# A kernel of cross-attention and experts: when two of its last eight batches are loaded, and which engine issues five of the final stores

## The chip, the cores and the metric

The kernel runs on one core of a Trainium2 chip, in one launch. The metric is the device time of that launch in microseconds (us). The engines of the core work side by side, each through its own list of instructions: TensorE (PE), VectorE (DVE), ScalarE (ACT), GpSimd (POOL) and SyncE (SP), which here only issues DMA transfers. ScalarE and GpSimd issue transfers too. An engine waits on semaphores, and what stands behind a waiting instruction in its list waits with it.

## The reference

The input x has 16 batches of 256 rows with 256 columns. First it gets cross-attention on a normalised x, then a layer of eight experts, of which each row uses two:

```python
x = x + xattn(layernorm(x), ctx, ctx, Wq, bq, Wk, bk, Wv, bv)
h = layernorm(x)                        # 4096 rows of 256
logits = h @ Wr.T + br                  # 8 experts
vals, idx = top_k(logits, 2); w = softmax(vals)
out = 0
for e in range(8):
    y = gelu(h @ W1[e].T + b1[e]) @ W2[e].T + b2[e]     # 256 -> 1024 -> 256
    out = out + (w where idx == e, summed)[:, None] * y
z = out + h
z = (z - mean(z)) * rsqrt(var(z) + 1e-12) * ln_w + ln_b  # per row
x = x + z
```

## The kernel before

**Stages.** Up to about 200 us the kernel does the attention batch by batch, normalises, routes each row to its two experts, and writes h to two tables in DRAM: `tokens_dram`, from which rows are gathered, and `sums_dram`, on which the experts' outputs are added. Then come 39 blocks (`BLOCKS`), each of 256 rows of one expert, seven of them with only 128. For each block GpSimd gathers its rows with an indirect DMA (`fetch`), TensorE multiplies by W1 (`up`) and W2 (`down`) with weights split in high and low halves, ScalarE applies the gelu, VectorE splits and scales, and GpSimd adds the rows of the result to `sums_dram` with two indirect DMAs, 128 rows each (`give`, L646 to L660), here called scatters. A block's scatters wait until those of the block before have landed (`scattered[0]` counts even blocks, `scattered[1]` odd ones; `landed(m, p)` is the count when all blocks of parity p ahead of pair m are there).

**The last normalisation.** A batch of 256 rows is complete when all blocks with rows of it have been added. The full blocks are taken in an order that goes by their first rows, so low batches are complete early: batches 0 to 7 (`ON_TIME` = 8) are loaded back, normalised and stored beside the last blocks (`load_early` and `store_early`, L503 to L511); an assertion at L256 bounds, with `OPEN`, how many seats can still be open. Batches 8 to 15 come after the last block. Their place `z_all` lies over the memory of w1hi.

**The tail, engine by engine.** SyncE waits for all down-products and all scatters (L530 to L532), issues eight loads, at most four in flight (L533 to L535), then the store of batch 7 (L536). VectorE measures mean and variance of two batches at a time (`measure_z`, L1462: four statistics at L1466, four aggregations at L1470). GpSimd makes a scale and a shift of them (`norm_pair`, L710: L712, L713, L715, L718). ScalarE applies them and writes to PSUM (`normal`, L1149, two instructions a batch). VectorE multiplies by ln_w (`weigh`, L1475) and x is added: for batches 8 to 12 (`HANDED` = 5) by GpSimd (`finish`, L722), for 13 to 15 by VectorE (`finish`, L1480). ScalarE issues all eight stores (L1158), each as soon as four more batches have been normalised, and the last four at the end; before each it waits for its batch's finish.

The order on each engine is written out by hand. GpSimd: `norm_pair` 0, 1, 2, finish 8, `norm_pair` 3, finish 9 to 12. VectorE: measure pairs 0, 1, 2, weigh 8 and 9, measure pair 3, weigh 10 to 13, then finish and weigh in turn.

Of the kernel before, what the change touches and what calls it, by code (L numbers as in the profile page):

```python
# [27 lines left out]
P = 128  # L28
# [5 lines left out]
def at_least(eng, sem, n):  # L34

    if not (isinstance(n, int) and n <= 0):
        eng.wait_ge(sem, n)
# [10 lines left out]
def build(nc, x, ctx_in, Wq, bq, Wk, bk, Wv, bv, Wr, br, W1, b1, W2, b2, ln_w, ln_b, out):  # L48
    NB, SQ, D = x.shape
    SK = ctx_in.shape[1]  # L50
    E, FF, _ = W1.shape
# [7 lines left out]
    BT = TB * P  # L59
    FULL = TOPK * TOK // BT  # L60
    SHORT = E - 1
    BLOCKS = FULL + SHORT
# [2 lines left out]
    PAIR_OF = E * PER_EXPERT // TB  # L65
    FAR = 1 << 20
    NOWHERE = 99
    OPEN = E * (BT - 1) + SHORT * P
    ON_TIME = 8
    ON_TIME_AT = 11  # L70
    HANDED = 5
# [9 lines left out]
    out_v = out.rearrange("b (j p) d -> p b j d", p=P)  # L81
# [6 lines left out]
    with ExitStack() as stack:  # L88
# [3 lines left out]
        def sem(name):  # L92
            return stack.enter_context(nc.semaphore(name))

        def sem2(name):
            return [sem(f"{name}{i}") for i in range(2)]
# [128 lines left out]
        z_all = w1hi[:, :].bitcast(F32).rearrange("p (b j d) -> p b j d", b=NB, j=TJ)  # L225
# [27 lines left out]
        HB = len(f_h)  # L253
        SETTLED = (FIRST + SHORT + 1) // 2
        assert ON_TIME_AT + ON_TIME == BLOCKS // 2
        for i in range(ON_TIME):  # L256
            assert 2 * SQ * (NB - i - 1) >= BT * (BLOCKS - 2 * (ON_TIME_AT + i) + 1) + OPEN

        def tiles(m, p):

            return 1 if isinstance(m, int) and FIRST <= 2 * m + p < FIRST + SHORT else TB

        def landed(m, p):

            if isinstance(m, int):
                return 16 * sum(tiles(i, p) for i in range(m))
            return 16 * TB * m - 16 * len([j for j in range(FIRST, FIRST + SHORT) if j % 2 == p])
# [76 lines left out]
        h_mm = sem("h_mm")  # L344
# [3 lines left out]
        y_mm = sem("y_mm")  # L348
        y_ready = sem("y_ready")
        y_self = sem("y_self")  # L350
        scattered = sem2("scattered")
# [7 lines left out]
        o_ready = sem("o_ready")  # L359
        last_done = sem("last_done")  # L360
        stored = sem("stored")
# [60 lines left out]
        def _(sp):  # L422
# [86 lines left out]
            def store_early(i):  # L509
                sp.wait_ge(early_done, i + 1)  # L510
                sp.dma_start(out_v[:, i, :, :], x1[:, i, :, :]).then_inc(stored, 16)  # L511
# [15 lines left out]
                if p == 1 and 0 <= m - ON_TIME_AT < ON_TIME - 1:  # L527
                    store_early(m - ON_TIME_AT)

            sp.wait_ge(y_mm, HB * BLOCKS)  # L530
            sp.wait_ge(scattered[0], landed(BLOCKS // 2 + 1, 0))
            sp.wait_ge(scattered[1], landed(BLOCKS // 2, 1))  # L532
            for b in range(ON_TIME, NB):  # L533
                at_least(sp, sums_loaded[b % 4], 16 * ((b - ON_TIME) // 4))
                sp.dma_start(z_all[:, b, :, :], sums_v[:, b, :, :]).then_inc(sums_loaded[b % 4], 16)  # L535
            store_early(ON_TIME - 1)  # L536
            sp.wait_ge(stored, 16 * NB)


        @block.gpsimd  # L540
        def _(pool):
# [168 lines left out]
            def norm_pair(q):  # L710
                pool.wait_ge(stats3, q + 1)
                nc.gpsimd.tensor_scalar(nmu3[:, q, :], mv3[:, q, :, 0], -1.0, None, ALU.mult)  # L712
                nc.gpsimd.tensor_scalar(ve3[:, q, :], mv3[:, q, :, 1], EPS_FFN, None, ALU.add).then_inc(norm3_self, 1)  # L713
                pool.wait_ge(norm3_self, 2 * q + 1)
                nc.gpsimd.tensor_tensor(scale3[:, q, :], ve3[:, q, :],  # L715
                                        minus_half[:, :, :].rearrange("p w j -> p (w j)"), ALU.pow).then_inc(norm3_self, 1)
                pool.wait_ge(norm3_self, 2 * q + 2)
                nc.gpsimd.tensor_tensor(shift3[:, q, :], nmu3[:, q, :], scale3[:, q, :], ALU.mult).then_inc(rn3_ready, 1)  # L718

            def finish(b):  # L720
                pool.wait_ge(zw_ready, b - ON_TIME + 1)
                nc.gpsimd.tensor_tensor(z_all[:, b, :, :], z_all[:, b, :, :], x1[:, b, :, :], ALU.add).then_inc(o_ready, 1)  # L722

            norm_pair(0)
            norm_pair(1)
            norm_pair(2)
            finish(ON_TIME)
            norm_pair(3)
            for b in range(ON_TIME + 1, ON_TIME + HANDED):
                finish(b)  # L730


# [265 lines left out]
        def _(act):  # L998
# [145 lines left out]
            def normal(b):  # L1144
                q = (b - ON_TIME) // 2
                act.wait_ge(rn3_ready, q + 1)
                for j in range(TJ):
                    i = TJ * (b % 2) + j
                    ins = nc.scalar.activation(bank[b - ON_TIME][:, j * D:(j + 1) * D], z_all[:, b, j, :], ACT.Identity,  # L1149
                                               bias=shift3[:, q, i:i + 1], scale=scale3[:, q, i:i + 1])  # L1150
                ins.then_inc(zn_ready, 1)

            def store(b):
                if b < ON_TIME + HANDED:
                    act.wait_ge(o_ready, b - ON_TIME + 1)
                else:
                    act.wait_ge(last_done, b - ON_TIME - HANDED + 1)
                act.dma_start(out_v[:, b, :, :], z_all[:, b, :, :]).then_inc(stored, 16)  # L1158

            for b in range(ON_TIME, NB):  # L1160
                normal(b)
                if b >= ON_TIME + 4:
                    store(b - 4)
            for b in range(NB - 4, NB):
                store(b)


# [1 line left out]
        def _(dve):  # L1169
# [292 lines left out]
            def measure_z(q):  # L1462
                for b in (ON_TIME + 2 * q, ON_TIME + 2 * q + 1):
                    dve.wait_ge(sums_loaded[b % 4], 16 * ((b - ON_TIME) // 4 + 1))
                    for j in range(TJ):
                        ins = nc.vector.bn_stats(st3[:, q, TJ * (b % 2) + j, :], z_all[:, b, j, :])  # L1466
                ins.then_inc(z_self, 1)
                dve.wait_ge(z_self, q + 1)
                for i in range(PT):
                    ins = nc.vector.bn_aggr(mv3[:, q, i, :], st3[:, q, i, :])  # L1470
                ins.then_inc(stats3, 1)

            def weigh(b):
                dve.wait_ge(zn_ready, b - ON_TIME + 1)
                nc.vector.tensor_tensor(z_all[:, b, :, :], bank[b - ON_TIME][:, :].rearrange("p (j d) -> p j d", j=TJ),  # L1475
                                        lnw_bc[:, :].unsqueeze(1).to_broadcast([P, TJ, D]), ALU.mult).then_inc(zw_ready, 1)

            def finish(b):
                dve.wait_ge(zw_ready, b - ON_TIME + 1)
                nc.vector.tensor_tensor(z_all[:, b, :, :], z_all[:, b, :, :], x1[:, b, :, :], ALU.add).then_inc(last_done, 1)  # L1480

            measure_z(0)
            measure_z(1)
            measure_z(2)
            weigh(ON_TIME)
            weigh(ON_TIME + 1)
            measure_z(3)
            for b in range(ON_TIME + 2, ON_TIME + HANDED + 1):
                weigh(b)
            for b in range(ON_TIME + HANDED, NB):  # L1490
                finish(b)
# [29 lines left out]
```

## Time and profile before

| what | value |
| --- | --- |
| time, median of 3 runs | 639.02 us (639.56, 634.88, 639.02) |
| the profiled execution, time | 636.95 us |
| its span, first to last instruction | 635.2 us |
| mean granted clock of TensorE | 0.944 |
| busy: TensorE, VectorE, ScalarE, GpSimd | 561.8, 435.9, 280.8, 318.8 us |
| the chain that ended last, by engine | PE 67%, DVE 13%, issue 6%, ACT 3%, DMA 2%, POOL 2% |

The profile is of one execution. Times in it count from the span's start. A timeline row gives the start, the length, the engine, the line of the kernel, the operation with what it writes and reads, and in brackets the idle time before it and what ended it. An engine name with a q (SPq, ACTq) is that engine's queue, where DMA issues stand: the row's length is that of the issue, not of the transfer. "Landing" is the time from issue to the last byte's semaphore. The chain of waits is followed back from the last instruction; each of its pieces is what the next one waited for.

### The profile page before, as it was taken

To read this page: it belongs to the slowest core of one execution; us is meant where nothing else is said; L and a number is where in the kernel's file an instruction comes from. 1 tells how busy PE (TensorE), PEld (TensorE's weight loads), DVE (VectorE), ACT (ScalarE), POOL (GpSimd) and SP (SyncE) were. 2 spreads that over 40 slices of the span, in tenths; PEclk is the share of its full clock that TensorE was granted. 3 is DMA by queue.
4 is the path that set the end of the run, shared out by engine and by line. 5 is a ranking of instruction groups with operands and counts; after the bars stand their busy time and mean duration, and the time that the engine had idled before them with its cause. 6 is when DMAs were issued, how large, how long until landed. Compare 5 with 4: busy or idle time off the path is not lost.

```text
span 635.2 us, 17704 instructions
## 1 busy us (share of the span) xinstructions
PE 561.8 (88%) x4878; PEld 493.8 (78%) x4879; DVE 435.9 (69%) x1320; ACT 280.8 (44%) x699; POOL 318.8 (50%) x524
## 2 busy tenths in 40 slices
PE   6999999997637999999999999999999999999700
PEld 5789988886526897668898989898898989898600
DVE  2479999998864476554676665757687777768546
ACT  1688877784324433334424333333435334442214
POOL 4024433443332245445454546456676667775446
PEclk9999999997658999999999999999999999999955
DMA  7356677664341133333242424343343445344354
GB/s 225 87 190 214 208 214 215 213 183 136 123 113 35 18 53 60 60 61 69 46 68 56 65 55 67 59 80 53 93 96 75 80 93 100 76 75 87 42 149 148
DMA packets 62402, 65.70 MB, mean 103 GB/s; under 512 B 10088, under 2 KB 58032, under 8 KB 62352
## 3 DMA queue, kind: packets, MB, share of 16 engines
q1 hardware_dynamic: 46544, 44.10, 22.7%
q0 software_dynamic: 13632, 18.91, 19.1%
q10 hardware_dynamic: 2176, 2.10, 1.0%
q8 instruction: 22, 0.36, 0.3%
q14 instruction: 28, 0.23, 0.1%
HBM read 43.07 MB, written 22.02 MB: 102 GB/s over the span
## 4 chain that ended last, share of the span: by engine, by line
PE 67%; DVE 13%; issue 6%; ACT 3%; DMA 2%; POOL 2%; DVEq 1%; POOLq 0%; SPq 0%; ACTq 0%
PE bank L925 11%; PE bank L927 10%; PE bank L926 10%; PE bank L949 10%; PE bank L951 9%; PE bank L950 9%; PE bank L904 3%; DVE w2hi L1250 2%; DVE st L1218 2%; DVE w2hi L1249 1%; DMA sums_dram<-xn,mt 1%; PE bank L783 1%; DVE w1lo L1192 1%; PE bank L871 1%; PE bank L877 1%
## 5 line engine op out<-in xcount | busy, mean ns | idle before, releaser
L1104 ACT ACTIVATE stage<-bank,mt 128x256 f32<-128x256 f32 (+1 forms) x312 | 122.2, 453 | 145.3 <-PE bank L927 142.5
L925 PE MATMUL bank<-xnt,w1hi 128*128 128x256 f16 (+1 forms) x624 | 165.4, 267 | 8.0 <-issue 3.5
L658 POOL DMA_INDIRECT sums_dram<-xn,mt x71 | 117.6, 1656 | 100.2 <-DVE xn L1377 81.7
L926 PE MATMUL bank<-xnt,w1hi 128*128 128x256 f16 (+1 forms) x624 | 164.6, 265 | 0.0
L927 PE MATMUL bank<-xnt,w1lo 128*128 128x256 f16 (+1 forms) x624 | 164.4, 265 | 0.0
L949 PE MATMUL bank<-w2hi,stage 128*128 x552 | 150.5, 273 | 0.2
L950 PE MATMUL bank<-w2lo,stage 128*128 x552 | 150.5, 273 | 0.0
L951 PE MATMUL bank<-w2hi,stage 128*128 x552 | 150.5, 273 | 0.0
L1362 DVE CAST stage<-stage 128x512 f16<-128x512 f32 (+1 forms) x156 | 64.9, 416 | 114.2 <-PE bank L951 111.2
L1364 DVE TENSOR_TENSOR stage<-stage 128x512 f16<-128x512 f32 (+1 forms) x156 | 100.6, 645 | 5.4
L639 POOL DMA_INDIRECT xg<-tokens_dram,mt x71 | 75.0, 1056 | 52.2 <-POOL mt L634 27.7
L925 PEld LDWEIGHTS bank<-xnt,w1hi 128*128 x624 | 61.3, 98 | 21.9 <-issue 10.9
L927 PEld LDWEIGHTS bank<-xnt,w1lo 128*128 x624 | 61.4, 98 | 6.6
L926 PEld LDWEIGHTS bank<-xnt,w1hi 128*128 x624 | 61.6, 99 | 6.2
L949 PEld LDWEIGHTS bank<-w2hi,stage 128*128 128x128 f16 x552 | 54.0, 98 | 7.7 <-issue 2.0
L950 PEld LDWEIGHTS bank<-w2lo,stage 128*128 128x128 f16 x552 | 54.0, 98 | 6.2
L951 PEld LDWEIGHTS bank<-w2hi,stage 128*128 128x128 f16 x552 | 54.0, 98 | 6.1
L1094 ACT CAST xnt<-bank 128x512 f16<-128x512 f32 (+1 forms) x39 | 21.4, 548 | 58.9 <-PE bank L904 58.9
L783 PE MATMUL bank<-ident,stage 128*128 128x128 f32 x256 | 43.1, 299 | 3.9 <-DVE w1lo L1192 2.4
L588 POOL TENSOR_SCALAR nmu<-mv 128x4 f32<-128x4 f32 (+1 forms) x19 | 4.6, 242 | 68.9 <-DVE mv L1231 59.1
L783 PEld LDWEIGHTS bank<-ident,stage 128*128 128x128 f32 x256 | 33.9, 155 | 6.6 <-DVE w1lo L1192 2.5
L634 POOL COPY mt<-mt 128x2 int32 (+1 forms) x39 | 31.3, 802 | 3.1 <-DVE wvt L1345 2.6
(226 smaller groups left out, 926.3 us busy)
## 6 DMA issues: line engine op xcount, KB each, us to landing
stage<-in_L_ffn_W_dram SPq DMA_DIRECT2D x16, 768.0 KB, 4.9
work<-in_L_ffn_b_dram SPq DMA_DIRECT2D x39, 128.0 KB, 2.9
x<-in_x_dram SPq DMA_DIRECT2D x16, 256.0 KB, 4.9
tokens_dram<-xn SPq DMA_DIRECT2D x16, 256.0 KB, 2.2
sums_dram<-xn SPq DMA_DIRECT2D x16, 256.0 KB, 2.8
stage<-in_L_ffn_W_dram SPq DMA_DIRECT2D x16, 256.0 KB, 3.6
work<-sums_dram SPq DMA_DIRECT2D x8, 256.0 KB, 3.3
out_dram<-x SPq DMA_DIRECT2D x8, 256.0 KB, 3.2
```

The lines of the kernel that those rows point to most:

```text
L639: nc.gpsimd.indirect_dma_start(out=xg[p][:, t, :], out_offset=None, in_=tokens_dram, in_offset=bass.IndirectOffsetOnAxis(ap=gidx[p][:, t:t ...
L658: nc.gpsimd.indirect_dma_start(out=sums_dram, out_offset=bass.IndirectOffsetOnAxis(ap=sidx[p][:, t:t + 1], axis=0), in_=y_sb[p][:, t, :], ...
L783: ins = nc.tensor.transpose(b_w[w][:, q * P:(q + 1) * P], stage[p][:, col:col + P], ident[:, :])
L925: nc.tensor.matmul(dst, w1hi[:, col], xhi[:, k, 0:bt], start=(k == 0), stop=False)
L926: nc.tensor.matmul(dst, w1hi[:, col], xlo[:, k, 0:bt], start=False, stop=False)
L927: ins = nc.tensor.matmul(dst, w1lo[:, col], xhi[:, k, 0:bt], start=False, stop=(k == KD - 1))
L949: nc.tensor.matmul(f_y[t], hhi[:, h], w2hi[:, col], start=(c == 0), stop=False)
L950: nc.tensor.matmul(f_y[t], hhi[:, h], w2lo[:, col], start=False, stop=False)
L951: ins = nc.tensor.matmul(f_y[t], hlo[:, h], w2hi[:, col], start=False, stop=(c == KF - 1))
L1104: ins = nc.scalar.activation(h32[:, c * bt:(c + 1) * bt], f_h[q][:, (c % 2) * bt:(c % 2 + 1) * bt], ACT.Gelu, bias=b1s[p][:, c:c + 1], sca ...
L1362: nc.vector.tensor_copy(hhi[:, s], h32[:, s]).then_inc(hhi_ready, 1)
L1364: nc.vector.tensor_tensor(hlo[:, s], h32[:, s], hhi[:, s], ALU.subtract).then_inc(split_ready, 1)
```

## The change

Batches 8 and 9 are loaded once all up-products are done and all blocks but the last have landed; the other six wait, as before, for the last block. The store of batch 7 moves between the two groups of loads. `OPEN` is smaller by one term of 255, and a new assertion says that the last block holds no row of batches 8 and 9. GpSimd and VectorE do the work of the pair of 8 and 9 first: GpSimd finishes 8 and 9 ahead of `norm_pair` 1, VectorE weighs 8 and 9 ahead of measuring pair 1, and weighs 10 and 11 ahead of measuring pair 3. The stores of batches 8 to 12 go from ScalarE's queue to SyncE's, after the loads. ScalarE normalises all eight batches and then issues the stores of 13 to 15.

```diff
--- before.py
+++ after.py
@@ -65,7 +65,7 @@
     PAIR_OF = E * PER_EXPERT // TB
     FAR = 1 << 20
     NOWHERE = 99
-    OPEN = E * (BT - 1) + SHORT * P
+    OPEN = (E - 1) * (BT - 1) + SHORT * P
     ON_TIME = 8
     ON_TIME_AT = 11
     HANDED = 5
@@ -253,6 +253,7 @@
         HB = len(f_h)
         SETTLED = (FIRST + SHORT + 1) // 2
         assert ON_TIME_AT + ON_TIME == BLOCKS // 2
+        assert 2 * SQ * (NB - ON_TIME - 2) >= BT + OPEN
         for i in range(ON_TIME):
             assert 2 * SQ * (NB - i - 1) >= BT * (BLOCKS - 2 * (ON_TIME_AT + i) + 1) + OPEN
 
@@ -527,13 +528,25 @@
                 if p == 1 and 0 <= m - ON_TIME_AT < ON_TIME - 1:
                     store_early(m - ON_TIME_AT)
 
-            sp.wait_ge(y_mm, HB * BLOCKS)
-            sp.wait_ge(scattered[0], landed(BLOCKS // 2 + 1, 0))
-            sp.wait_ge(scattered[1], landed(BLOCKS // 2, 1))
-            for b in range(ON_TIME, NB):
+            def load_z(b):
                 at_least(sp, sums_loaded[b % 4], 16 * ((b - ON_TIME) // 4))
                 sp.dma_start(z_all[:, b, :, :], sums_v[:, b, :, :]).then_inc(sums_loaded[b % 4], 16)
+
+            def store(b):
+                sp.wait_ge(o_ready, b - ON_TIME + 1)
+                sp.dma_start(out_v[:, b, :, :], z_all[:, b, :, :]).then_inc(stored, 16)
+
+            sp.wait_ge(h_mm, HB * BLOCKS)
+            sp.wait_ge(scattered[0], landed(BLOCKS // 2, 0))
+            sp.wait_ge(scattered[1], landed(BLOCKS // 2, 1))
+            load_z(ON_TIME)
+            load_z(ON_TIME + 1)
             store_early(ON_TIME - 1)
+            sp.wait_ge(scattered[0], landed(BLOCKS // 2 + 1, 0))
+            for b in range(ON_TIME + 2, NB):
+                load_z(b)
+            for b in range(ON_TIME, ON_TIME + HANDED):
+                store(b)
             sp.wait_ge(stored, 16 * NB)
 
 
@@ -722,11 +735,13 @@
                 nc.gpsimd.tensor_tensor(z_all[:, b, :, :], z_all[:, b, :, :], x1[:, b, :, :], ALU.add).then_inc(o_ready, 1)
 
             norm_pair(0)
+            finish(ON_TIME)
+            finish(ON_TIME + 1)
             norm_pair(1)
             norm_pair(2)
-            finish(ON_TIME)
+            finish(ON_TIME + 2)
             norm_pair(3)
-            for b in range(ON_TIME + 1, ON_TIME + HANDED):
+            for b in range(ON_TIME + 3, ON_TIME + HANDED):
                 finish(b)
 
 
@@ -1151,17 +1166,12 @@
                 ins.then_inc(zn_ready, 1)
 
             def store(b):
-                if b < ON_TIME + HANDED:
-                    act.wait_ge(o_ready, b - ON_TIME + 1)
-                else:
-                    act.wait_ge(last_done, b - ON_TIME - HANDED + 1)
+                act.wait_ge(last_done, b - ON_TIME - HANDED + 1)
                 act.dma_start(out_v[:, b, :, :], z_all[:, b, :, :]).then_inc(stored, 16)
 
             for b in range(ON_TIME, NB):
                 normal(b)
-                if b >= ON_TIME + 4:
-                    store(b - 4)
-            for b in range(NB - 4, NB):
+            for b in range(ON_TIME + HANDED, NB):
                 store(b)
 
 
@@ -1480,12 +1490,14 @@
                 nc.vector.tensor_tensor(z_all[:, b, :, :], z_all[:, b, :, :], x1[:, b, :, :], ALU.add).then_inc(last_done, 1)
 
             measure_z(0)
+            weigh(ON_TIME)
+            weigh(ON_TIME + 1)
             measure_z(1)
             measure_z(2)
-            weigh(ON_TIME)
-            weigh(ON_TIME + 1)
+            weigh(ON_TIME + 2)
+            weigh(ON_TIME + 3)
             measure_z(3)
-            for b in range(ON_TIME + 2, ON_TIME + HANDED + 1):
+            for b in range(ON_TIME + 4, ON_TIME + HANDED + 1):
                 weigh(b)
             for b in range(ON_TIME + HANDED, NB):
                 finish(b)
```

## Rows read from the trace of the kernel before

**Rows 1.** The chain that ended last: start us, length us, what it was.

```profile
600.02 3.81 DMA sums_dram<-xn,mt
...
606.92 3.83 DMA sums_dram<-xn,mt
...
611.85 3.98 DMA w1hi<-sums_dram
...
622.67 0.21 POOL w1lo L712
...
625.71 0.38 ACTq L1158
...
626.14 1.06 ACT bank L1149 x2
...
629.76 1.04 DVE w1hi L1480
```

**Rows 2.** Timeline of GpSimd, tail: start us, length us, engine, line, operation [idle before].

```profile
606.92 1.55 POOL L658 DMA_INDIRECT sums_dram<-xn,mt  x1 [0.30 <-issue]
...
615.59 0.25 POOL L712 TENSOR_SCALAR w1lo<-w1lo 128x4 f32<-128x4 f32 x1 [7.13 <-DVE w1lo L1470]
...
624.42 1.26 POOL L722 TENSOR_TENSOR w1hi<-w1hi,x 128x512 f32<-128x512 f32 x1
...
625.64 1.71 POOL L722 TENSOR_TENSOR w1hi<-w1hi,x 128x512 f32<-128x512 f32 x1
```

**Rows 3.** Timeline of VectorE, tail.

```profile
604.10 0.69 DVE L1416 TENSOR_TENSOR x<-x,work 128x512 f32<-128x512 f32 x1
...
613.67 1.42 DVE L1466 BATCH_NORM_STATS2 w1lo<-w1hi 128x6 f32<-128x256 f32 x4 [8.88 <-DMA w1hi<-sums_dram]
...
615.12 0.38 DVE L1470 BATCH_NORM_AGGREGATE w1lo<-w1lo 128x2 f32<-128x6 f32 x4
...
619.35 1.26 DVE L1475 TENSOR_TENSOR w1hi<-bank,ctx_sb 128x512 f32<-128x512 f32 x2
...
625.00 1.23 DVE L1480 TENSOR_TENSOR w1hi<-w1hi,x 128x512 f32<-128x512 f32 x1
...
627.95 1.17 DVE L1480 TENSOR_TENSOR w1hi<-w1hi,x 128x512 f32<-128x512 f32 x1
```

**Rows 4.** Timeline of ScalarE, tail.

```profile
617.49 2.04 ACT L1149 ACTIVATE bank<-w1hi,w1lo 128x256 f32<-128x256 f32 x4 [25.27 <-POOL w1lo L718]
```

**Rows 5.** Timeline of SyncE's and ScalarE's DMA issues.

```profile
588.52 0.34 SPq L501 DMA_DIRECT2D work<-in_L_ffn_b_dram  x1
...
610.91 6.01 SPq L535 DMA_DIRECT2D w1hi<-sums_dram  x8
...
611.35 0.46 SPq L535 DMA_DIRECT2D w1hi<-sums_dram  x1
...
616.97 0.47 SPq L511 DMA_DIRECT2D out_dram<-x  x1
...
631.77 0.51 ACTq L1158 DMA_DIRECT2D out_dram<-w1hi  x1
```

**Rows 6.** GpSimd's scatters (L658) in the loop, 400 to 600 us.

```profile
L658 POOL DMA_INDIRECT sums_dram<-xn,mt x37: 1558/1695/1948, 402.1 to 598.2; - x37
...
DMA to landing us min/median/max: 3.7/4.0/4.8
```

**Rows 7.** Landing of a block's two scatters at 447.2 and 449.2 us, store issued 447.5.

```profile
DMA to landing us min/median/max: 4.5/4.5/4.5
...
DMA to landing us min/median/max: 3.9/3.9/3.9
```

**Rows 8.** Landing of the loop's loads of sums (L507).

```profile
DMA to landing us min/median/max: 2.8/3.3/4.7
```

**Rows 9.** Landing of ScalarE's last five stores (L1158).

```profile
DMA to landing us min/median/max: 2.1/2.5/3.0
```

**Rows 10.** Windows: us, busy us of each engine (count), clock, DMA share, GB/s.

```profile
632.00:634.00 2.00, 0.00 (x0) 0.00 (x0) 0.00 (x0) 0.00 (x0) 0.00 (x0) 0.50 1.02 342
```

## The prediction

> **What bounds the kernel now.** I read the page's chain first, then the timeline of each engine over the last 45 us, then the DMA landings. TensorE carries 67% of the chain and stops at 602 us; nothing before that is touched by the change. What it touches is the tail after it, 33 us long. The chain [rows 1] shows its joints: the scatter of the last block but one lands at 603.83, the last scatter at 606.92 + 3.83 = 610.75, and only then are the eight loads issued. The third load lands at 615.84. GpSimd's normalising follows, held up by a finish (pair 3 starts at 622.67), then ScalarE's issue of a store at 625.71 with the two normalisations of one batch behind it, then VectorE's last finish, ending at 629.76 + 1.04 = 630.80. The last store is issued at 631.77 [rows 5], and the span ends at 635.17. The reader should see two things. Three engines stand idle around the wait: GpSimd 7.13 us to 615.59, VectorE 8.88 us to 613.67, ScalarE 25.27 us to 617.49 [rows 2 to 4]. And ScalarE's queue mixes stores that wait with normalisations that others wait for.
>
> Below, "pair 0" is batches 8 and 9, pair 1 is 10 and 11, and so on. All times are on the axis of the profile of before.
>
> **Loading pair 0 early.** Its wait (603.83) comes 6.92 us before the old one (610.75). The up-products, which read the memory that the loads overwrite, have long ended, so the wait on them costs nothing. SyncE took 0.16 us from landing to issue before (610.75 to 610.91 [rows 5]), so load 8 goes out at 603.99 and load 9 about 0.44 later, at 604.43 (610.91 to 611.35). Before, load 8 landed when the measuring of pair 0 began, 613.67 - 610.91 = 2.76 us after issue [rows 3, 5]; load 9 within 3.0, since the measuring ran on without a gap. The same kind of load in the loop took 2.8 to 4.7, median 3.3 [rows 8]. I take 3.0, the end nearest in place: load 9 lands at 607.4.
>
> From there pair 0 goes on by the rows of before: measuring ended at 615.50, 1.17 after load 9; GpSimd's four small instructions with the hand-over to ScalarE 1.90 (615.59 to 617.49 [rows 2, 4]); ScalarE's two batches 2.04; the second weighing 0.63 (1.26 for two [rows 3]). With the other hand-overs, some 0.15, the last weighing ends 5.9 us after load 9 lands, at 613.3. GpSimd has its second scatter issued by 608.47 [rows 2], in time for the normalising at 608.6. Queued behind pair 0 on VectorE is the measuring of pair 1, which has its data at 613.67, where pair 0 had it before. So pair 0 fits with 0.35 us to spare, and GpSimd's finishes of 8 and 9 end by about 614.8, before pair 1's means are there (615.50). **Cost nothing**, with that cover; if load 9 takes the 4.7 us, VectorE is 1.3 us late.
>
> **What the earlier traffic does to the last scatter.** Two loads and the store of batch 7 (which moves up from 616.97 [rows 5] to about 604.95) run beside it. In the loop a scatter beside which such a store was issued landed in 4.5 us, and the second scatter of that block, issued 2 us later, in 3.9 [rows 7]; scatters in general took 3.7 to 4.8 [rows 6], the last one 3.83. All three transfers are issued by 605.4, about 1.5 us before the second scatter's issue begins (606.92), which is the one that ends last. I take no delay, with 0 to 1.0 as bounds.
>
> VectorE now measures while GpSimd issues the second scatter. That instruction took 1.55 us with VectorE idle [rows 2] and 1.70 in the median, 1.95 at most, in the loop with VectorE at work [rows 6]. I take +0.15, bounds 0 to 0.4. The Trainium skill (SBUF — State Buffer, Who interferes with whom) says that a VectorE instruction with one SBUF input outside its two-port modes does not contend with GpSimd; by it this term would be 0 and the gain 0.15 larger. The trace of before cannot say: in the loop VectorE runs other instructions beside the scatters.
>
> **The rest of the tail, three pairs instead of four.** Load 10 takes the place of 8, and so on. Measuring: pair 1 from 613.67 to 615.50, 1.83, pair 2 from 615.86, when its load lands, to 617.7. GpSimd: pair 1 to 617.45, pair 2 to 619.65, finish of 10 to 620.9. ScalarE: 10 and 11 from 617.49 to 619.53, 12 and 13 to 621.8. VectorE weighs 10 and 11 when ScalarE gives them, to 620.2, and only then measures pair 3 (1.42 + 0.38 [rows 3]), to 622.0. So pair 3's means come only 0.6 earlier than GpSimd took them up before (622.67), but no finish and no store stands in their way any longer: GpSimd is done with them at 623.9, and ScalarE, whose queue holds no store until all eight batches are normalised, starts batch 14 at 623.95 instead of 626.14 (14 and 15 end at 626.0). VectorE meanwhile weighs 12 and 13 and finishes 13, to about 624.2.
>
> Then the finishes collide. The same 128x512 addition takes VectorE 0.69 with GpSimd not adding (604.10 [rows 3]), but 1.23 and 1.17 beside GpSimd's finishes: GpSimd's of 624.42 ends at 625.68, VectorE's at 626.23, 0.55 later; GpSimd's next one then took 1.71 instead of 1.26 [rows 2, 3]. So each waits for the other. GpSimd's finishes of 11 and 12 run from 624.2 to about 626.9; VectorE weighs 14 by about 625.9, its finish waits and ends 0.55 after GpSimd's, at 627.5; weighing 15 to 628.1; its finish, now alone, 0.69: **628.7 to 628.8**, against 630.80. Gain 2.1. The slack of 0.35 and the collisions together could move this by 0.5 either way.
>
> The trace of before has no two-input addition on VectorE beside GpSimd's small instructions; finish 13 would stand there now. Bounds: 0, or one addition, 0.69. I took 0.3, near the middle, in the times above. The Trainium skill's page (same section) has it that the later of two such instructions is blocked until the earlier ends; the collisions of the finishes agree with it; by it the term is up to 0.69, and the gain 0.4 smaller.
>
> **The stores.** Batches 8 to 12 leave ScalarE's queue for SyncE's, behind the six loads; behind them stands only SyncE's wait for the end. On ScalarE the last store waited from 630.80 to 631.77, behind four others: 0.97, of which about 0.9 goes. From its issue to the span's end took 3.40 us, with four stores (1 MB) in flight at 342 GB/s [rows 10]; the last five took 2.1 to 3.0 to land [rows 9]. Now the last five are issued at about 625.7, 626.1, 626.9, 627.5 and 628.8. At 342 GB/s one takes 0.77 us, so the last meets little in front of it. I take 0.4 off, bounds 0 to 0.8.
>
> **Sum.** -2.1 (last finish) - 0.9 (issue) - 0.4 (landing) + 0.15 (scatter's issue) = **-3.25 us**, about 0.5%. Against the profiled execution (636.95, 1.75 around its span of 635.2) that gives 633.7. This execution lies 2.1 us under the median of three, 639.02, and between the lowest and the highest of them; I put the forecast on the middle of the four times, (636.95 + 639.02) / 2 = 638.0, hence **634.7**.
>
> **Rivals.**
> (a) The loads land late or the scatter is held up: one of the bounds of 1.0 and 1.3 holds. For it: a load in the loop took 4.7, scatters up to 4.8. Against: most of these loads took about 3.3. Gain 1.0 to 2.2, time 636 to 637.
> (b) The means of pair 3 set the end whatever comes before: they gain only 0.6, and if the collisions eat the rest and the stores still queue, the gain is 0.6, time 637.4. Against it: batch 14 waited for a store, not for its means (it began at 626.14 [rows 1], while GpSimd had left the means for its next finish at 624.42 [rows 2]).
> (c) Slower: the order is turned round. VectorE must weigh 8 and 9 before it measures pair 1, and GpSimd must finish them before it normalises pair 1. If pair 0 is not early, its whole chain lies open: each us of load 9 after 607.75 costs one, and beyond 611.0 (6.6 us after issue) the change loses. If it landed at 614.3, as before, the cost would be 6.5 and the net +3.3: 641.3. Against it: no such load took over 4.7.
> (d) The change does not do what it says, because SyncE comes to the new wait late. Its last issue before that wait stands at 588.52 [rows 5], so this has hardly a chance; the time would be as in (c).
>
> **How the numbers follow.** Forecast 0.75, (a) 0.13, (b) 0.07, (c) with (d) 0.05. The runs of before alone spread over 634.88 to 639.56. The forecast's own range is this spread less 3.3: 631.6 to 636.3. Rivals (a) and (b) take it to 638.4. A measurement of this kernel can tell about 1% (6.4 us) from no change; no case but chance brings a gain so large, and (c) brings half such a loss. Faster by over 1%: 0.09, within 1%: 0.88, slower by over 1%: 0.03.
>
> **What would show it.** Right: two load issues at 604.0 to 604.5, far from the other six; measuring of pair 0 at about 607; the last scatter landing within 0.3 of where it did; no ScalarE idle time put down to a GpSimd finish; the last VectorE finish 18 us after the last scatter's landing instead of 20.05; the last store issued within 0.2 of it. Wrong: measuring of pair 1 waiting for a weighing of batch 9 instead of its load; a last scatter of over 4.5; ScalarE's batch 14 waiting for pair 3's means until after 625; or the last stores landing over 3 us after issue.

## The result and the profile after

Median 629.98 us (20 runs, 625.95 to 635.31) against 635.19 for the kernel before in 20 runs (630.23 to 639.56). The ratio is 0.9942, 95% interval 0.992 to 0.9963: 3.7 us less, between 2.4 and 5.1. The forecast of 3.25 us less lies inside; the time forecast, 634.7, and its range from 631.6 do not hold 629.98, because the kernel before itself runs at 635.19 and not at the 638.0 from which the gain was taken off.

The profiled execution of the changed kernel took 635.14, span 633.4, only 1.8 under the profiled one of before. Two things of opposite sign are in that: its last scatter starts at 609.36 instead of 606.92 [rows 2], 2.44 later, in code that the change does not touch; and from there to the span's end it takes 24.00 us instead of 28.25. I call this stretch the **tail** from here on. In the tail the change is worth 4.25 us.

Lines of the engines in the changed kernel are 10 to 15 higher than before: L533 issues the loads, L537 and L1170 the stores, L671 is the scatter, L1476 the measuring, L1485 and L1490 VectorE's weighing and finish, L735 GpSimd's finish, L1164 the normalisation. The chain that ended last, after (start us, length us, what); it answers to [rows 1]:

```profile
602.42 3.84 DMA sums_dram<-xn,mt
...
609.36 3.84 DMA sums_dram<-xn,mt
...
613.21 2.94 DMA w1hi<-sums_dram
...
619.99 2.05 ACT bank L1164 x4
...
622.75 1.32 DVE w1lo L1476 x4
...
626.46 0.44 ACT bank L1164
...
628.28 1.14 DVE w1hi L1490
...
630.05 0.69 DVE w1hi L1490
```

No GpSimd finish and no store issue stands in it any more. One pair waits for its data (613.21), is normalised (619.99), weighed, and pair 3 is measured (622.75) and normalised; then come VectorE's finishes, the last ending at 630.74. Timeline of SyncE's issues (start, length, line, what):

```profile
606.35 0.90 SPq L533 DMA_DIRECT2D w1hi<-sums_dram  x2
...
613.21 4.00 SPq L533 DMA_DIRECT2D w1hi<-sums_dram  x6
...
617.25 12.01 SPq L537 DMA_DIRECT2D out_dram<-w1hi  x5
```

Two loads leave at 606.35, 0.09 us after the last block but one has landed (602.42 + 3.84, chain), then the store of batch 7, six loads from 613.21, and the five stores. Timelines of VectorE, GpSimd and ScalarE, to be read against [rows 2 to 5]:

```profile
609.17 1.50 DVE L1476 BATCH_NORM_STATS2 w1lo<-w1hi 128x6 f32<-128x256 f32 x4 [1.96 <-DMA w1hi<-sums_dram]
...
616.17 1.43 DVE L1476 BATCH_NORM_STATS2 w1lo<-w1hi 128x6 f32<-128x256 f32 x4 [0.35 <-DMA w1hi<-sums_dram]
...
625.68 0.69 DVE L1490 TENSOR_TENSOR w1hi<-w1hi,x 128x512 f32<-128x512 f32 x1
...
628.28 1.14 DVE L1490 TENSOR_TENSOR w1hi<-w1hi,x 128x512 f32<-128x512 f32 x1
```

```profile
609.36 1.55 POOL L671 DMA_INDIRECT sums_dram<-xn,mt  x1 [0.31 <-issue]
...
625.08 1.04 POOL L728 TENSOR_TENSOR w1lo<-w1lo,minus_half 128x4 f32<-128x4 f32 x1
626.19 0.24 POOL L731 TENSOR_TENSOR w1lo<-w1lo 128x4 f32<-128x4 f32 x1
...
626.38 2.48 POOL L735 TENSOR_TENSOR w1hi<-w1hi,x 128x512 f32<-128x512 f32 x2
```

```profile
626.46 0.57 ACT L1164 ACTIVATE bank<-w1hi,w1lo 128x256 f32<-128x256 f32 x1 [2.16 <-POOL w1lo L731]
...
629.45 1.71 ACTq L1170 DMA_DIRECT2D out_dram<-w1hi  x2
```

Pair 0 is measured at 609.17, while GpSimd issues the second scatter, which takes 1.55 as before; pair 1 at 616.17, as soon as its load lands. VectorE's finish of 13 takes 0.69, that of 14 takes 1.14 beside GpSimd's finishes, and the last one is alone and takes 0.69 (chain). ScalarE's batch 14 waits 2.16 for GpSimd's means, and for no store.

How the program closes is told by the rows of the line that ends it (L88: engine, operation, count, length in ns, start in us). Before, after, and in the run with the stores moved alone, told below:

```profile
L88 POOLq DRAIN  x1: 10275/10275/10275, 624.2 to 624.2; - x1
...
L88 SPq COMPARE_BRANCH  x1: 41/41/41, 634.8 to 634.8; - x1
```

```profile
L88 POOLq DRAIN  x1: 6972/6972/6972, 626.2 to 626.2; - x1
L88 DVEq DRAIN  x1: 732/732/732, 630.1 to 630.1; - x1
...
L88 SPq COMPARE_BRANCH  x1: 41/41/41, 632.9 to 632.9; - x1
```

```profile
L88 POOLq DRAIN  x1: 10723/10723/10723, 621.2 to 621.2; - x1
...
L88 SPq COMPARE_BRANCH  x1: 41/41/41, 629.9 to 629.9; - x1
```

GpSimd's closing drain ends at 624.24 + 10.28 = 634.51 before, 4.27 us after its last finish (624.42 + 5.83 = 630.25). After, it ends at 633.13, again 4.27 after its last finish (626.38 + 2.48 = 628.86). In all thirteen profiles the span ends 0.23 after the drain or 0.36 after SyncE has seen the last store land (its branch, after 632.95 + 0.04), whichever is later. Before it was the store (drain 634.51, branch 634.80). After, the two are level: 633.13 + 0.23 and 632.99 + 0.36. This drain was in no term of the forecast.

### The profile page after: what moved, and what is told of

It is laid out like the page before. It is cut to its first block, busy times and chain, and to the rows that moved or that the text cites. A ratio compares the mean times of both kernels' runs of the same rounds, so it can differ in the third digit from the quotient of the medians.

```text
span 633.4 us, 17704 instructions
## 1 busy us (share of the span) xinstructions
PE 564.5 (89%) x4878; PEld 495.9 (78%) x4879; DVE 435.6 (69%) x1320; ACT 280.8 (44%) x699; POOL 318.2 (50%) x524
## 4 chain that ended last, share of the span: by engine, by line
PE 67%; DVE 13%; issue 6%; ACT 4%; DMA 2%; POOL 1%; DVEq 1%; POOLq 0%; ACTq 0%
PE bank L940 11%; PE bank L942 10%; PE bank L941 10%; PE bank L964 10%; PE bank L966 9%; PE bank L965 9%; PE bank L919 3%; DVE w2hi L1260 2%; DVE st L1228 2%; DVE w2hi L1259 1%; DMA sums_dram<-xn,mt 1%; PE bank L798 1%; DVE w1lo L1202 1%; PE bank L886 1%; PE bank L892 1%
## 5 line engine op out<-in xcount | busy, mean ns | idle before, releaser
L671 POOL DMA_INDIRECT sums_dram<-xn,mt x71 | 117.6, 1657 | 100.5 <-DVE xn L1387 82.0
```

The costliest lines, as they stand in the source:

```text
L671: nc.gpsimd.indirect_dma_start(out=sums_dram, out_offset=bass.IndirectOffsetOnAxis(ap=sidx[p][:, t:t + 1], axis=0), in_=y_sb[p][:, t, :], ...
```

## The experiments

Tails, and within them the end of GpSimd's last finish and of VectorE's (us from the start of the last scatter's issue), with the ratio to the kernel before where it was timed. The expectations tell tails from the scatter's landing, 3.5 to 3.8 us less. The tails are of one profile each.

| run | GpSimd | VectorE | tail | ratio (95%) |
| --- | --- | --- | --- | --- |
| before | 23.33 | 23.88 | 28.25 | |
| e4_before_again | 23.04 | 23.58 | 27.95 | 1.0032 (1.0004 to 1.006) |
| after | 19.50 | 21.38 | 24.00 | 0.9942 (0.992 to 0.9963) |
| e11_after_again | 19.21 | 21.09 | 23.70 | 0.9945 (0.9915 to 0.9975) |
| e1_early_only | 19.75 | 21.63 | 24.67 | 0.9938 (0.9917 to 0.996) |
| e2_stores_only | 23.64 | 22.53 | 28.14 | 1.0002 (0.9978 to 1.0026) |
| e3_pair0_late | 25.58 | 27.46 | 30.07 | 1.0011 (0.9985 to 1.0037) |
| e5_old_order | 21.99 | 20.87 | 26.48 | |
| e6_stores_handed4 | 23.21 | 23.76 | 27.71 | |
| e7_handed4 | 18.17 | 21.37 | 23.97 | |
| e8_measure_first | 18.83 | 19.38 | 23.32 | |
| e9_first_six_handed4 | 18.85 | 20.72 | 23.34 | 0.9919 (0.9887 to 0.9951) |
| e10_first_handed4 | 17.27 | 20.48 | 23.08 | 0.9909 (0.9877 to 0.9942) |

In eight of the thirteen the tail is GpSimd's column plus 4.50 (drain 4.27 and 0.23), within 0.01. In the other five (before twice, e1, e7, e10) it is longer, and the last store ends it.

**The kernel before again (e4_before_again),** with no edit.

> The kernel before, once more, for the level of its time and for what differs between executions of the same code. Theory 1 (the level is set by when TensorE's clock comes back between 180 and 220 us, ahead of all changed code): ratio 1.00 within its interval, tail 24.4 within 0.2 us, and the last scatter lands at another time than 610.75 by as much as the stretch from 180 to 220 us was longer or shorter. Rival (the level depends on the code, and the three runs shown were a fair sample): median near 639, last scatter at 610.8.

Its tail agrees within 0.3 (28.25, 27.95). Its timed ratio, 1.0032 with an interval that leaves out 1, says how far a ratio of two identical programs can stray here (1.00 within the interval had been expected): differences of 0.3% in time are not read below. Tails are, where rows show what makes the difference. Its last scatter started at 606.84, hardly elsewhere than in the first profile, by two differences that cancel (last section).

**Early loads alone (e1_early_only).** The stores go back into ScalarE's queue, in the places of before:

```diff
-            for b in range(ON_TIME, ON_TIME + HANDED):
-                store(b)
             sp.wait_ge(stored, 16 * NB)
...
             for b in range(ON_TIME, NB):
                 normal(b)
+                if b >= ON_TIME + 4:
+                    store(b - 4)
-            for b in range(ON_TIME + HANDED, NB):
+            for b in range(NB - 4, NB):
                 store(b)
```

> The two early loads and the new orders on GpSimd and VectorE, but all eight stores issued by ScalarE in the old places. In what follows the tail is the stretch from the landing of the last scatter to the span's end: 24.4 us in the kernel before, 20.2 in the changed one. Theory 1 (the early pair makes nearly all of the gain; the finishes come early enough that ScalarE's stores hold nothing up): tail 20.2 to 20.8, time 0.55 to 0.65% under before. Theory 2 (taking the stores out of ScalarE's queue is a large part): ScalarE's batches 14 and 15 wait for stores again, tail 21.5 to 23.

Tail 24.67, from the landing 20.9 and just over the first theory's range: early pair and new orders bring 3.58 of the 4.25, and the time cannot be told from the changed kernel's. VectorE's measuring of batch 11, its last finish and ScalarE's last stores here:

```profile
612.69 0.75 DVE L1479 BATCH_NORM_STATS2 w1lo<-w1hi 128x6 f32<-128x256 f32 x2 [0.69 <-DMA w1hi<-sums_dram]
...
625.89 0.69 DVE L1493 TENSOR_TENSOR w1hi<-w1hi,x 128x512 f32<-128x512 f32 x1
```

```profile
624.73 2.26 ACTq L1171 DMA_DIRECT2D out_dram<-w1hi  x4
```

The last finish ends at 626.58 and the four stores end at 626.99 with the last issue 0.38 long, so it starts 0.03 after the finish. The 0.97 us that the last store waited before is gone without moving a store: finishes that come earlier had emptied the queue. Of the 0.67 to the changed kernel's tail, 0.25 stands at VectorE's last finish already: measuring pair 1 waited 0.69 for the load of batch 11, where in the changed kernel it ran through (616.17, 1.43). The other 0.42 lies behind that finish (3.04 to the end, 2.62 in the changed kernel), and that is what moving the stores brought.

**Stores alone (e2_stores_only).** Loads and orders of before, SyncE and ScalarE as in the changed kernel. In short:

```diff
+            for b in range(ON_TIME, ON_TIME + HANDED):
+                store(b)
             sp.wait_ge(stored, 16 * NB)
...
             for b in range(ON_TIME, NB):
                 normal(b)
-                if b >= ON_TIME + 4:
-                    store(b - 4)
-            for b in range(NB - 4, NB):
+            for b in range(ON_TIME + HANDED, NB):
                 store(b)
```

> Only the stores move: batches 8 to 12 stored by SyncE after the loads, ScalarE normalises all eight batches before it stores; loads and orders on GpSimd and VectorE as in the kernel before. Theory 1: batch 14 on ScalarE starts at the means of pair 3 instead of behind a store, some 1.7 us earlier, but GpSimd's four finishes, which come after pair 3, then end last: tail 22.4 to 23.2 (before 24.4), time 0.2 to 0.3% under before. Theory 2 (the stores are the larger part): tail 21.5 or less. Theory 3 (nothing): 24.4.

Tail 28.14, no gain, the third theory, though VectorE's last finish is 1.35 earlier than before (22.53 against 23.88). GpSimd's finishes of 9 to 12:

```profile
621.38 6.28 POOL L729 TENSOR_TENSOR w1hi<-w1hi,x 128x512 f32<-128x512 f32 x4
```

They end at 627.66, the last store has landed by 629.91, when SyncE branches, and the span ends at 632.2, because GpSimd's drain (rows above) ends at 631.93, 4.27 after its last finish. What the moved stores gave VectorE, GpSimd's four finishes after the means of pair 3 and this drain took back.

**Orders without early data (e3_pair0_late).**

```diff
-            load_z(ON_TIME)
-            load_z(ON_TIME + 1)
             store_early(ON_TIME - 1)
             sp.wait_ge(scattered[0], landed(BLOCKS // 2 + 1, 0))
-            for b in range(ON_TIME + 2, NB):
+            for b in range(ON_TIME, NB):
                 load_z(b)
```

> The changed kernel, but batches 8 and 9 are loaded after the last scatter with the other six. The prediction's case (c): VectorE and GpSimd must carry pair 0 to its end before they take pair 1, so its chain lies open, 5.9 us from the landing of its second load instead of none: tail 20.2 + 6.5 = 26.7, 2.3 us over the kernel before (0.36% slower). Rival: the new order costs less, since the later pairs' data is then there without waits and GpSimd and VectorE catch up: tail 24.4 or less.

Tail 30.07, 26.3 from the landing: 1.8 us worse than before where 2.3 was expected. VectorE measures pair 0, weighs 9, and only then measures pair 1:

```profile
611.73 1.46 DVE L1474 BATCH_NORM_STATS2 w1lo<-w1hi 128x6 f32<-128x256 f32 x4 [8.50 <-DMA w1hi<-sums_dram]
...
617.66 0.69 DVE L1483 TENSOR_TENSOR w1hi<-bank,ctx_sb 128x512 f32<-128x512 f32 x1 [0.29 <-ACT bank L1162]
...
618.26 1.40 DVE L1474 BATCH_NORM_STATS2 w1lo<-w1hi 128x6 f32<-128x256 f32 x4
```

Pair 1 is measured 6.5 us after pair 0, at 618.26, right behind the weighing of 9; in the kernel before it followed after 2.2, when its load had landed (613.67 to 615.84 [rows 1, 3]). The prediction's case (c) is a real mechanism, and it is the early data that kept it from deciding. The time (1.0011) is too near 1 to show it.

**Early data with the old orders (e5_old_order).** GpSimd and VectorE as before; GpSimd's part of the edit:

```diff
             norm_pair(0)
-            finish(ON_TIME)
-            finish(ON_TIME + 1)
             norm_pair(1)
             norm_pair(2)
-            finish(ON_TIME + 2)
+            finish(ON_TIME)
             norm_pair(3)
-            for b in range(ON_TIME + 3, ON_TIME + HANDED):
+            for b in range(ON_TIME + 1, ON_TIME + HANDED):
```

> The changed kernel (early loads, stores by SyncE) with the old orders on GpSimd and VectorE: the means of pairs 0, 1, 2, then finish 8, means of pair 3, finishes 9 to 12. Theory 1 (early data alone is not the gain; GpSimd must also spend it on finishing 8 and 9 early): GpSimd still has four finishes after the means of pair 3, the last ends about 18.3 us after the last scatter's landing, and the tail is 22.5 to 23.2 us. Rival (early data is enough): tail 20.2 to 21.

Tail 26.48, 22.8 from the landing, as the first theory has it. GpSimd's finishes:

```profile
617.57 1.27 POOL L735 TENSOR_TENSOR w1hi<-w1hi,x 128x512 f32<-128x512 f32 x1
...
620.59 6.28 POOL L735 TENSOR_TENSOR w1hi<-w1hi,x 128x512 f32<-128x512 f32 x4
```

One finish, then the means of pair 3, then four finishes to 626.87, with the drain to 631.1. So of the 4.25 us, 2.5 hang on the orders (26.48 to 24.00), and neither half brings it alone: the orders without the data lose, the data without the orders brings 1.8 even with the stores moved.

**GpSimd's share.** `HANDED` 5 to 4 in the run with the stores alone (e6_stores_handed4) and in the changed kernel (e7_handed4):

```diff
-    HANDED = 5
+    HANDED = 4
```

> As the run with the stores moved alone, whose tail was 24.4, but GpSimd finishes batches 8 to 11 and VectorE 12 to 15. Theory 1 (the span ends 4.3 us after GpSimd's last finish plus 0.24 where this is later than the last store, since GpSimd's closing drain takes so long; that ate the gain of moving the stores): one finish less, tail 22.5 to 23.1. Rival (the stores behind SyncE's waits cost it): tail 24 or more.

Tail 27.71, 24.0 from the landing: a miss, where the rival stood, though not by its cause. The drain still ended 4.27 after the last finish and set the end (23.21 + 4.50). But that finish came only 0.43 earlier than in e2: three finishes take 1.67 less than four (4.61, 6.28), and they began 1.24 later in the tail (18.61 instead of 17.37). Two things made them late. GpSimd's rows come first, then VectorE's:

```profile
622.93 0.61 POOL L725 TENSOR_TENSOR w1lo<-w1lo 128x4 f32<-128x4 f32 x1
...
623.50 4.61 POOL L729 TENSOR_TENSOR w1hi<-w1hi,x 128x512 f32<-128x512 f32 x3
```

```profile
622.80 0.69 DVE L1482 TENSOR_TENSOR w1hi<-w1hi,x 128x512 f32<-128x512 f32 x1
```

GpSimd's last small instruction took 0.61 instead of 0.20 beside VectorE's finish of 12, ending 0.05 after it. The other 0.82 came with the data of pair 1: its first load, a piece of the chain in both runs, took 3.89 in e2 and 4.83 here, though the edit does not touch it.

```profile
608.88 3.89 DMA w1hi<-sums_dram
```

```profile
609.71 4.83 DMA w1hi<-sums_dram
```

So most of the miss is a late load; without it the tail would have been about 23.2 from the landing, just over the expected range (an estimate: 24.0 less 0.82).

> The changed kernel, GpSimd finishing batches 8 to 11 and VectorE 12 to 15. In the changed kernel GpSimd's drain and SyncE's last landing end together. Theory 1 (both bind, and VectorE's finish of 14 waits for GpSimd's of 12): without the finish of 12 on GpSimd both ends move, tail 19.6 to 20.0 against 20.2. Rival (VectorE has no room for one more finish): tail 20.5 or more.

Tail 23.97, 20.2 from the landing: another miss, between the two ranges. GpSimd's drain moved 1.34 earlier, but VectorE's last finish stayed (21.37, 21.38), and the last store sets the end. In the changed kernel VectorE waited 1.18 for ScalarE's batch 14; here the added finish fills that wait, and the finish of 13, which meets GpSimd's of 11, takes 1.70 (the changed kernel's one meeting took 1.14):

```profile
621.80 1.70 DVE L1490 TENSOR_TENSOR w1hi<-w1hi,x 128x512 f32<-128x512 f32 x1
```

**Pair 3 measured first (e8_measure_first),** since the chain after runs through its measuring behind the weighing of 10 and 11:

```diff
             measure_z(2)
-            weigh(ON_TIME + 2)
-            weigh(ON_TIME + 3)
             measure_z(3)
-            for b in range(ON_TIME + 4, ON_TIME + HANDED + 1):
+            for b in range(ON_TIME + 2, ON_TIME + HANDED + 1):
                 weigh(b)
```

and on GpSimd `finish(ON_TIME + 2)` behind `norm_pair(3)`.

> The changed kernel, but VectorE measures pair 3 before it weighs batches 10 and 11, and GpSimd makes its means before it finishes 10. The changed kernel's chain runs through the measuring of pair 3 waiting for weighing 11. Theory 1: the means of pair 3 are ready 2.3 us sooner, the finishes then collide more, GpSimd's last ends 14.6 us after the scatter's landing: tail 18.9 to 19.4 against 20.2. Rival (the data of pair 3 lands too late to gain from it): tail 20 or more.

Tail 23.32, 19.6 from the landing (19.4 at most was expected). VectorE's measuring of pair 3 and its last finish, and the closing rows:

```profile
620.89 1.37 DVE L1475 BATCH_NORM_STATS2 w1lo<-w1hi 128x6 f32<-128x256 f32 x4
...
628.75 1.04 DVE L1489 TENSOR_TENSOR w1hi<-w1hi,x 128x512 f32<-128x512 f32 x1
```

```profile
L88 POOLq DRAIN  x1: 8755/8755/8755, 624.7 to 624.7; - x1
...
L88 SPq COMPARE_BRANCH  x1: 41/41/41, 632.2 to 632.2; - x1
```

The last finish is 2.0 us earlier in the tail than after (19.38 against 21.38), but only 0.7 reaches the end (0.6 counted from the landing): GpSimd's drain ends at 633.50, SyncE saw the last store at 632.24.

**Putting it together.** e9 adds to e8 six loads in flight, each with a semaphore of its own, and `HANDED` 4; e10 is e8 with `HANDED` 4 alone. Of the edit of e9, beside what is told, SyncE's part (VectorE's waits go with it):

```diff
             def load_z(b):
-                at_least(sp, sums_loaded[b % 4], 16 * ((b - ON_TIME) // 4))
-                sp.dma_start(z_all[:, b, :, :], sums_v[:, b, :, :]).then_inc(sums_loaded[b % 4], 16)
+                sp.dma_start(z_all[:, b, :, :], sums_v[:, b, :, :]).then_inc(sums_loaded[b - ON_TIME], 16)
```

> The changed kernel with pair 3 measured before the weighing of 10 and 11, all six late loads in flight at once, and GpSimd finishing 8 to 11, VectorE 12 to 15. Theory (the tail is bound by the work of GpSimd and VectorE after pair 3's measuring, and by GpSimd's drain): tail 18.2 to 18.9 us against 20.2 of the changed kernel and 24.4 of the kernel before, time 0.85 to 0.95% under before. Rival (six loads share the bandwidth, pair 1 comes later): tail 20 or more, time as the changed kernel's.

Tail 23.34, 19.6 from the landing: nothing over e8, between theory and rival. GpSimd's drain set the end again (18.85 + 4.50). With all six in flight the later ones take longer to land, as the rival had it, but pairs 2 and 3 paid for it, not pair 1. The first load of pair 3, in the chain:

```profile
607.44 5.94 DMA w1hi<-sums_dram
```

In the changed kernel the loads took up to 4.5. So VectorE began to measure pair 3 11.65 us into the tail; in e10, with four in flight, at 10.59.

> The changed kernel with pair 3 measured before the weighing of 10 and 11 (as in the run that did this alone, four loads in flight) and GpSimd finishing only 8 to 11. From here on a tail is told from the start of the last scatter's issue, which every trace has: 28.25 us before, 24.00 in the changed kernel, 23.32 with pair 3 measured first, where GpSimd's drain set the end and the last store landed 1.3 us earlier. Theory (with one finish less on GpSimd the stores set the end): tail 22.3 to 22.8, time 0.8 to 0.95% under before. Rival (VectorE gets the finish and ends as much later): tail 23.2 or more.

Tail 23.08: 0.6 to 0.9 under the changed kernel's two, and less than expected. VectorE's finish of 12 and its last one:

```profile
619.67 1.57 DVE L1489 TENSOR_TENSOR w1hi<-w1hi,x 128x512 f32<-128x512 f32 x1
...
624.88 0.69 DVE L1489 TENSOR_TENSOR w1hi<-w1hi,x 128x512 f32<-128x512 f32 x1
```

The added finish met GpSimd's and took 1.57, so VectorE's last came 1.1 later than in e8; now the stores set the end (17.27 + 4.50 would be 21.77). Timed, 0.9909 stands beside 0.9945 for the changed kernel on the same chip, with intervals that overlap: the shorter tail is seen in the profile, the shorter time is likely but not shown.

> The changed kernel once more, beside the other on the same chip. Theory: tail 24.0 within 0.3 (the kernel before, run twice, gave 28.25 and 27.95), ratio to before between 0.992 and 0.996; the start of the last scatter, which took 601.8 to 610.4 us in the profiles so far with the same code ahead of it, may lie anywhere in that range. Rival: the tail differs between executions as much as the start does.

Tail 23.70 and ratio 0.9945, both as expected. The 0.3 to the first profile is the last scatter's landing, 3.52 here and 3.84 there; from the landing both take 20.2. The two second profiles give the change the same 4.25 (27.95 to 23.70). Here the last scatter started at 605.61, 3.75 us before that of the first profile of the same code.

## Why the prediction was wrong

**The step that failed is the level:** "I put the forecast on the middle of the four times, (636.95 + 639.02) / 2 = 638.0", and the range made from the spread of three of them. Over 20 runs the kernel before has its median at 635.19, and in the later sets of runs at 634.65, 637.15 and 634.81. Of the 4.7 us between 634.7 and 629.98, 2.8 are this level. Off 635.19 the forecast gain gives 631.9, inside the range but still 2.0 over 629.98; the medians of the two sets are 5.2 apart, more than their ratio gives. Executions of this program spread over 9 us; four of them do not fix its median to 3 us, and the range took the spread of three for all there was. Two of these three proved to be the slowest of the twenty. That was bad luck; building the level and the range on them was the error.

**The gain** was forecast as 3.25, is 3.7 (2.4 to 5.1) in the timed runs and 4.25 in the profiles. Step by step, times after shifted back by 2.44:

- Loads of pair 0 at 603.99: 603.91. Measuring at about 607: 606.73. Pair 1's measuring unhindered: its load released it. Right.
- The last scatter: no delay taken, 3.84 against 3.83. Right. Its issue: +0.15 taken, 1.55 both times. The term was 0, as the Trainium skill's rule had it for a VectorE instruction with at most one SBUF input outside its two-port modes (SBUF — State Buffer, Who interferes with whom).
- VectorE's last finish: 2.1 forecast, 2.50 measured (23.88 to 21.38). The 0.3 charged for a finish beside GpSimd's small instructions was not paid: VectorE's finish took its 0.69, GpSimd's instruction 0.24 instead of 0.20. And GpSimd's finishes of 11 and 12 took 2.48, not the 2.7 of the forecast (624.2 to 626.9). The rule of the same section of the Trainium skill, that the later of the two is blocked until the earlier ends, agrees with the rows only in part. GpSimd's instruction, which began at 626.19, ended just after VectorE's finish did (626.37), and the one of e6, where the finish ended 0.56 after it had begun, took 0.61. But GpSimd's instruction ahead of it (625.08, 1.04 long) was running when VectorE's finish began at 625.68, and that finish was not held up.
- Stores, 0.9 and 0.4: the stretch from the last finish to the end fell from 4.37 to 2.62, 1.75. The wait for the issue fell by 0.94 (0.97 to 0.03), as forecast, but from the last issue to the end it fell by 0.81 (3.40 to 2.59), so the landing term was half its size. The reason was wrong too: the early pair frees the queue (e1). Moving the stores brings 0.4 of tail on top of that, and nothing without it (e2).
- Not foreseen: GpSimd's drain. It did not bind before (0.4 to spare) and just binds after, so it cost the forecast nothing; it is what would have broken a larger one.

The three terms that were off, 0.40, 0.15 and 0.45, make the 1.0 between 3.25 and 4.25.

Rivals (a) and (d) did not come about. Of (c), the mechanism is real (e3) but its condition did not occur. Of (b), the means of pair 3 are indeed in the chain after, yet the end moved.

## What to carry to other kernels

Moving data earlier pays when the in-order queues behind it are reordered to spend it: here the orders alone lost 1.8 us, the early data under old orders kept less than half. Before claiming gain at a kernel's end, find every engine's close there, not only the last store: the next one may be a few tenths of a microsecond behind. And forecast a small change as a difference; give the level of the time the spread that single executions have.

## What was not expected of the hardware

**GpSimd closes 4.27 us after its last addition.** In all thirteen profiles the drain ended 4.27 us after GpSimd's last finish, whether that came 17.3 or 25.6 us into the tail. VectorE's drain ended 0.05 after VectorE's last. The finish itself was over: in the changed kernel SyncE issued the store that waits for it at 628.89, 0.03 after its end. Why GpSimd's drain takes so long, no run here shows.

**Where executions of the same code differ.** The last scatter started between 601.76 and 610.41 us in the thirteen profiles, and from the first scatter to the last it took only 388.4 to 389.7: the differences arise before the first block is added. The windows show it (us, busy us of TensorE, its weight loads, VectorE, ScalarE and GpSimd with counts, then the granted clock, DMA share, GB/s), for before, after and e2:

```profile
160.00:180.00 20.00, 9.75 (x60) 7.45 (x58) 16.28 (x82) 4.47 (x9) 4.74 (x17) 0.59 0.44 134
...
180.00:190.00 10.00, 4.70 (x19) 3.42 (x20) 5.01 (x11) 3.68 (x6) 4.97 (x9) 0.50 0.40 107
...
190.00:210.00 20.00, 16.43 (x123) 13.45 (x122) 7.46 (x14) 8.95 (x21) 4.44 (x6) 0.86 0.10 28
```

```profile
190.00:210.00 20.00, 16.44 (x101) 12.74 (x100) 7.46 (x14) 7.53 (x17) 4.44 (x6) 0.69 0.11 28
```

```profile
190.00:210.00 20.00, 16.44 (x134) 13.94 (x132) 9.32 (x18) 8.72 (x20) 2.92 (x6) 0.91 0.08 22
```

In all three the clock is at the lower of its two levels (0.50, 1.2 GHz) from 180 to 190; before that, in the first, TensorE was busy 9.75 of 20 us. How much of the stretch from 190 to 210 is at 2.4 GHz differs: TensorE is busy 16.4 us of it each time, with 123, 101 and 134 matmuls done. The first scatter, before and after:

```profile
218.45 1.65 POOL L658 DMA_INDIRECT sums_dram<-xn,mt  x1 [7.22 <-DVE xn L1377]
```

```profile
220.87 1.65 POOL L671 DMA_INDIRECT sums_dram<-xn,mt  x1 [7.21 <-DVE xn L1387]
```

It starts 2.42 later after, and that is the 2.44 that the last one starts later. From the attention's first exponential to the first scatter it took 195.2 to 195.4 us in the three profiles with a mean clock of 0.76 or less between 190 and 210, 192.3 to 192.7 in nine with 0.86 to 0.91, and 190.5 in e9, where the clock was already higher from 180 to 190 (0.59). That the clock is the cause is argued from these rows; no run changed it alone. A second part arises at the start: that first exponential, before and in e4,

```profile
25.81 0.36 ACT L1048 ACTIVATE work<-bank,least 128x120 f32<-128x120 f32 x1 [0.82 <-DVE least L1207]
```

```profile
22.90 0.36 ACT L1048 ACTIVATE work<-bank,least 128x120 f32<-128x120 f32 x1 [0.82 <-DVE least L1207]
```

is 2.91 us apart in the same code. In e4 the stretch from there to the first scatter, one of the three with the lower clock, was 2.80 longer and took that back. Each of the two is over half of what this change is worth, which is why its worth shows in the tail and not in one time.
